# The second pair of banks of a direct band: read by ScalarE, ahead of its seed, and no longer by VectorE

## The reference, cut to what matters

```python
xn  = _gn(x)                                  # group norm, 32 groups of 2 channels
res = conv3x3(xn, W_id, b_id)                 # 3x3, 64 -> 64 channels, every image
# once, from xn[0]: wavelet bands, two attentions, 3x3 convolution of 256 channels
out = leaky_relu(conv3x3(dmt, W_enc, b_enc), 0.01)
x   = x + out + res
```

## Time and profile before

| | before |
|---|---|
| timed, median of 3 | 1817.76 us |
| the profiled execution | 1814.87 us |
| its span | 1813.1 us |
| TensorE busy | 1761.4 us (97%) |
| VectorE busy | 1450.2 us (80%) |
| ScalarE busy | 1238.6 us (68%) |
| GpSimd busy | 545.5 us (30%), all but a few us of it before the images |
| granted TensorE clock, mean | 0.994 |
| moved by DMA | 391.84 MB, 216 GB/s |

### The profile page before, as it was taken

The page is one execution under the profiler, slowest core; times in us unless marked ns, Lnnn a source line. Parts: engine busy times, 40 slices in busy tenths (PEclk is TensorE's granted clock), DMA queues, the critical chain, the costliest instruction groups (busy, mean ns, idle before and its releaser), DMA issues. The chain is left out here.

```text
span 1813.1 us, 69228 instructions
## 1 busy us (share of the span) xinstructions
PE 1761.4 (97%) x31540; PEld 1470.2 (81%) x31540; DVE 1450.2 (80%) x1926; ACT 1238.6 (68%) x1339; POOL 545.5 (30%) x365
## 2 busy tenths in 40 slices
PE   9999999999999999989999999999999999999997
PEld 9997999999999999965577797767966756967676
DVE  5665578778777887668989889888889888888886
ACT  5555666666666666667776777767776767766774
POOL 0005788888888888640000000000000000000000
PEclk9999999999999999999999999999999999999999
DMA  8884399888888888458998998998989989989994
GB/s 186 245 296 126 122 274 227 212 219 216 212 215 215 215 215 206 100 125 204 235 234 223 239 239 226 240 240 229 238 224 236 247 213 232 242 219 230 249 234 140
DMA packets 132964, 391.84 MB, mean 216 GB/s; under 512 B 49884, under 2 KB 50656, under 8 KB 118464
## 3 DMA queue, kind: packets, MB, share of 16 engines
q1 hardware_dynamic: 132672, 387.43, 82.7%
HBM read 258.88 MB, written 128.45 MB: 214 GB/s over the span
## 5 line engine op out<-in xcount | busy, mean ns | idle before, releaser
L1766 PE MATMUL ps<-big,tail 64*64 64x448 f16 x3840 | 323.3, 353 | 11.8 <-DVE ps L1961 7.8
L1766 PE MATMUL ps<-pool_of 64*64 64x448 f16 x5184 | 302.5, 352 | 7.9 <-DVE pool_of L1625 4.2
L1766 PE MATMUL ps<-pool_of,tail 64*64 64x448 f16 x4896 | 300.1, 349 | 0.7 <-issue 0.7
L1766 PE MATMUL ps<-big,pool_of 64*64 64x448 f16 x3552 | 278.5, 352 | 17.1 <-DVE ps L1961 11.9
L1292 DVE BATCH_NORM_STATS2 pool_of<-big 128x6 f32<-128x448 f32 x392 | 232.2, 616 | 76.4 <-DMA big<-in_x 76.3
L1766 PEld LDWEIGHTS ps<-pool_of 64*64 64x64 f16 x5184 | 196.2, 107 | 68.0 <-issue 10.1
L1766 PEld LDWEIGHTS ps<-pool_of,tail 64*64 64x64 f16 x4896 | 189.6, 106 | 59.3 <-issue 1.3
L1066 PE MATMUL ps<-pool_of 112*128 112x246 f16 x1344 | 218.8, 271 | 1.7 <-DVE pool_of L1280 0.8
L1070 PE MATMUL ps<-pool_of 112*128 112x168 f16 x1344 | 217.8, 243 | 0.0
L1766 PEld LDWEIGHTS ps<-big,tail 64*64 64x64 f16 x3840 | 169.0, 107 | 57.9 <-DVE ps L1961 10.4
L1069 PE MATMUL ps<-pool_of 112*128 112x90 f16 x1344 | 201.3, 206 | 0.0
(11 more groups left out here) (252 smaller groups left out, 3809.8 us busy)
## 6 DMA issues: line engine op xcount, KB each, us to landing
out<-tail SPq DMA_DIRECT2D x448, 224.0 KB, 3.6
big<-in_x SPq DMA_DIRECT2D x392, 224.0 KB, 5.2
pool_of<-in_x SPq DMA_DIRECT2D x139, 560.0 KB, 7.4
tail<-in_x SPq DMA_DIRECT2D x69, 560.0 KB, 7.4
pool_of<-row_filtered SPq DMA_DIRECT2D x110, 224.0 KB, 4.0
row_filtered<-big SPq DMA_DIRECT2D x2, 6272.0 KB, 22.8
pool_of<-in_x SPq DMA_DIRECT2D x30, 392.0 KB, 7.1
row_filtered<-big SPq DMA_DIRECT2D x4, 1568.0 KB, 9.2
```

Source lines behind the costliest of these rows:

```text
L1766: mm = pe.matmul(psum[bank + r][C * k:C * k + C, 0:NT], wt[i % 2][lanes, h, s, kx, :], v[u][lanes, rows_of(k), kx:kx + W], start=False, st ...
```

## The change

```diff
@@ -1522,7 +1522,7 @@
         banks_set = sem(top, "banks_set")
         g_seeded = sem(top, "g_seeded")
         g_done = sem(top, "g_done")
-        g_read = sem(top, "g_read")
+        g_read = [sem(top, f"g_read{g}") for g in range(2)]
         a_seeded = sem(top, "a_seeded")
         m2_done = sem(top, "m2_done")
         twice_ready = sem(top, "twice_ready")
@@ -1629,7 +1629,7 @@
 
             i, b = direct(j)
             if j:
-                act.wait_ge(g_read, 2 * j - 1 + g)
+                act.wait_ge(g_read[g], j)
             act.activation(g_bank[g], e_rows[:, :, b, g, :, :].rearrange("p r q w -> p r (q w)"), ACT.Identity,
                            scale=lane(r_out, i), bias=lane(mean_r, i)).then_inc(g_seeded, 1)
 
@@ -1834,7 +1834,8 @@
                                      stage[p][C * k:C * k + C, s, :, :].rearrange("c g n -> c (g n)")).then_inc(stored[p], 16)
 
             def store_direct(j):
-                sp.wait_ge(g_read, 2 * j + 2)
+                for g in range(2):
+                    sp.wait_ge(g_read[g], j + 1)
                 store(*direct(j), 0)
 
             def store_minimal(j):
@@ -1885,6 +1886,13 @@
                     act.wait_ge(stored[1], 64 * j)
                 act.activation(stage[1][:, :, :, 0:W], a_bank.rearrange("p r (g w) -> p r g w", g=2), ACT.Identity,
                                scale=lane(m_out, i)).then_inc(even_read, 1)
+
+            def read_second(j):
+                i, b = direct(j)
+                if j:
+                    act.wait_ge(stored[0], 64 * j)
+                act.wait_ge(g_done, 2 * j + 2)
+                act.activation(stage[0][:, :, 1, :], g_bank[1], ACT.Identity, scale=lane(m_out, i)).then_inc(g_read[1], 1)
 
             def seed_minimal(j):
                 i, b = minimal(j)
@@ -1911,6 +1919,8 @@
                     even_rows(q)
                 if q + 1 < NW:
                     seed_minimal(q + 1)
+                if q + 1 < ND:
+                    read_second(q + 1)
                 if q + 2 < ND:
                     seed_direct(act, q + 2, 1)
 
@@ -1919,6 +1929,8 @@
 
                 i, b = minimal(j)
                 k = place_w(j)
+                if j:
+                    dve.wait_ge(sums_split, j)
                 landed(dve, k)
                 if b == BOTTOM:
                     dve.wait_ge(filled, fill_of(i, b))
@@ -1946,12 +1958,12 @@
                 dve.scalar_tensor_tensor(v_lo[:, 0:R, 1:1 + W], xs[place_w(j) % XS][:, 0:R * W].rearrange("p (r w) -> p r w", w=W),
                                          norm_all[:, i, 0:1], v_hi[:, 0:R, 1:1 + W], ALU.mult, ALU.subtract).then_inc(split_done, 1)
 
-            def read_direct(j, g):
+            def read_first(j):
                 i, b = direct(j)
                 if j:
                     dve.wait_ge(stored[0], 64 * j)
-                dve.wait_ge(g_done, 2 * j + g + 1)
-                dve.tensor_scalar(stage[0][:, :, g, :], g_bank[g], lane(m_out, i), None, ALU.mult).then_inc(g_read, 1)
+                dve.wait_ge(g_done, 2 * j + 1)
+                dve.tensor_scalar(stage[0][:, :, 0, :], g_bank[0], lane(m_out, i), None, ALU.mult).then_inc(g_read[0], 1)
 
             def seed_odd(j):
                 dve.wait_ge(m1_done, j + 1)
@@ -1981,7 +1993,7 @@
                 if i + 1 < B and b in DIRECT[2:4]:
                     build_part(dve, i + 1, DIRECT.index(b) - 2)
                 if q + 1 < ND:
-                    read_direct(q + 1, 0)
+                    read_first(q + 1)
                 if q >= 0 and q + 2 < ND:
                     split(dve, q + 2)
                 if q >= 0:
@@ -1989,8 +2001,6 @@
                 if q + 1 < NW:
                     differences(q + 1)
                     sums_low(q + 1)
-                if q + 1 < ND:
-                    read_direct(q + 1, 1)
             odd_rows(NW - 1)
 
         def tensor(pe):
```

## The result

The changed kernel takes 1833.88 us (median of 4 runs, 1831.45 to 1835.08), the kernel before 1818.16 in the same session (4 runs, 1817.34 to 1818.73). The ratio is 1.0086, with a 95% interval of 1.0065 to 1.0106: slower by 15.7 us, where +8.6 was forecast. The profiled execution took 1831.45 us, 16.6 more than the one of before.

What follows compares the result with a forecast made beforehand. TensorE bounds plain periods; in build periods the chain through ScalarE and VectorE to `seed_odd` delays it. 7.4 + 1.0 − 1.2 + 0.6 + 0.8 = +8.6 us, a median of 1826.4, range 1820.5 to 1833.5.

Steps and rivals of the forecast that it cites:

- The read on ScalarE: Pair 1's read, moved into ScalarE's order behind `even_rows`, was to take a step of 1.05 us.
- Build periods: TensorE's gaps before `product_m0`: first build periods 0.81 to 1.86 (+7.4 us), second ones 1.96 to 2.10 (+1.0 us).
- About 7: Build-period sum in us, instead of 8.4, if twice as many of TensorE's stalls fall into build periods.
- First and last period: Loop's first period: earlier seed, −1.2 us; last period: later `diffs_high` and `double`, TensorE waiting, +0.6 us.
- The clock: Stretches at 1.2 GHz behind second build gaps, 1.5 us each: 3.5 against 3, +0.8 us; none behind gaps of 1.86.
- Plain periods: 0: In periods without builds the chain moves 1.05 us, 0.65 of 1.70 in hand are left, TensorE loses 0.
- The period from 1119.01: Recorded plain period with a late seed, 3.05 us after its start; 17.23 us long, TensorE busy throughout; cited for 0 cost.
- TensorE's own stalls: Stalls behind which no engine stands, 8.7 us in 12 places; no term of the sum, only able to hide gaps.
- Stores land late: Rival, slower: VectorE's read of pair 0 waits for direct bands' stores, 12 us over plain periods, near 1838; chance 0.07.
- VectorE's own length: Rival, faster: VectorE's work between `seed_odd` steps sets build gaps, so relief gives −18.3 us, near 1799.5; chance 0.06.
- Own stalls hide it: Rival, no difference: longer build-period gaps swallow about 4 us of TensorE's stalls, near 1820; chance 0.09.
- the clock behind nearly all gaps: Rival, slower: 11 more slow clock stretches behind the 14 build gaps, 16.5 us in place of 0.8, near 1842; chance 0.07.

Runs made afterwards that it cites:

- The second recordings: The kernel before and the changed kernel, each run once more unaltered: 1818.3 us and 1829.6 us.

## Why the prediction was wrong in size

The sign and the mechanism on the chain were right; the size was not, and the time fell 0.4 us above the range. Step by step:

- *The read on ScalarE*, 1.05: measured 1.03.
- *Build periods*, 0.81 to 1.86 and 1.96 to 2.10: measured 1.87 and 2.08. In sum +6.8 instead of +8.4, as more of these gaps were hidden in part: the second one of 1.19 us at 994.94 comes after a stretch of the slow clock, the first one of 0.89 at 1485.67 after an own stall of 0.77. "About 7" was given for that case.
- *First and last period*, −1.2 and +0.6: −0.9 and +0.4.
- *The clock*, +0.8: +1.5 with one stretch more. One of the four stands behind a first build gap of 1.87, for which the forecast took none, since 1.94 was the shortest that it had seen followed by one. The second recordings, with none and two, show that one execution doesn't give the size of this term.
- *Plain periods: 0* is the step that failed: with no builds, so with plain periods alone, the changed kernel is 8.3 us slower, and 5.1 of it are own stalls. The argument was that 1.05 of the 1.70 us in hand are used and TensorE doesn't see it. That holds for `seed_odd`: with no builds there is one wait of 1.2 us, at the end, in both kernels. It says nothing of what else hangs on the seed of pair 1 and the read before it: the stores. The period from 1119.01, which "lost nothing", was one case with late stores, and one case isn't enough: without builds 27 of 55 periods of the changed kernel are longer than 17.15 us, and 14 of the other.
- *TensorE's own stalls* were named and taken as fixed, as something that can only hide a gap. They were a term: +6.7 of 16.6. The trace had what it took to see this: the stalls' releaser is no engine, and the DMA view has the packets of code.
- *The rivals.* "Stores land late" looked at the right event and the wrong victim. VectorE waits 1.7 us in all for their landing; what is hurt is TensorE's code. "VectorE's own length" fell: its wait at the head of the chain rose from 94.8 us in all to 148.1, as the lines below show. The Trainium skill, Perfetto Trace Analysis, section Optimizing Scalar/DVE Operations, which the prediction weighed, says that such a move may make sense for a VectorE that is saturated. At this place VectorE is not: it waits for ScalarE, now 2.90 us in a plain period, and relieving it brought no gain that a run shows. The same read ahead of `even_rows` did pay, since ScalarE is idle there. "Own stalls hide it" had the sign of their effect the wrong way round, and "the clock behind nearly all gaps" would have needed eleven more stretches where there is one.

The waits of VectorE that speak against "VectorE's own length", before and after:

```profile
DVE tail L1946 <- ACT big L1863: 94.8, 55, 1.9
...
DVE tail L1958 <- ACT big L1864: 148.1, 53, 3.0
```

## What to carry to other kernels

Work that moves to another engine is priced by its place in that engine's order: the same read costs 15.7 us behind `even_rows`, on the chain, and gains 16 ahead of it, in a wait. Idle time of TensorE that no engine ends is not a constant; look in the DMA view for its code, and ask of every change what it does to the times of loads and stores, even if it leaves their number alone. Here the late packets stood behind loads, so the loads are the first thing to look at. "It is in hand" must be asked for every consumer of the delayed instruction, the store queue among them.

## What the runs showed of the hardware that was not expected

- TensorE's code comes in 16 KB packets over the DMA engines that carry the data, and these reach a share of 0.94 in a plain period. With 153 and 154 packets the own stalls of the kernel before ranged from 1.3 to 31.8 us by the times of SyncE's issues alone.
- One line that delays loads (`b_seeded`) made the kernel before 10.4 us faster, to 1807.89 (ratio 0.9922 to 0.9962).
- A profiled execution differs from another of the same kernel ahead of the images: the first `even_rows` started at 830.53 us in one of the kernel before and at 838.31 in the other. From the first to the last `even_rows` these two took 974.0 and 969.7 us, the changed kernel 992.6 and 987.8. What is worth a few us is better read from the stage than from the total.
